# A mixture-of-experts kernel whose per-tile expert weights are copied by VectorE instead of by SyncE's transfers

## The chip, the cores and the metric

The kernel runs on one NeuronCore of one Trainium2 chip. The metric is the device time of one launch in microseconds. The kernel before has three timed runs: 1335.67, 1336.54 and 1336.85 us, a median of 1336.54.

## The reference, cut to what matters

Six layers work on a residual stream x of 4096 tokens with 128 features, in float32: a mixture of experts with gelu, a state-space layer, the gelu mixture again, a mixture with swiglu, an attention layer of the RWKV kind, and the swiglu mixture again. The changed code is that of the mixtures:

```
gelu mixture   (8 experts, 2 of them for each token, F = 512):
  h      = gelu(x @ w1[e] + b1[e])          w1[e]: 128 x 512
  y      = h @ w2[e] + b2[e]                w2[e]: 512 x 128
swiglu mixture (8 experts, 2 of them for each token, I = 256):
  h      = silu(x @ w1[e].T) * (x @ w3[e].T)   both 128 x 256 as the kernel holds them
  y      = h @ w2[e].T                         256 x 128
each: out = sum over a token's two experts of gate * y
```

The kernel computes only the two chosen experts of a token.

## The kernel before

**Mixtures.** `mixture` is called three times: for the first gelu layer, for the second gelu layer and the first swiglu layer together (the merged layer: a gelu stage, then a swiglu stage), and for the last swiglu layer. Each stage cuts its 32 groups of 128 tokens into four parts (of 4, 12, 12, 4 groups in the first layer; 4, 12, 8, 8 and 8, 12, 8, 4 in the merged one; 8, 12, 8, 4 in the last). For each part VectorE normalises the tokens (`stats`, `normalise`), TensorE computes the gate's logits, VectorE picks two experts for each token and computes a place for each token and choice in a sorted list (`route`, `places`), and GpSimd sends the tokens to their places in DRAM, one indirect transfer of 128 rows for each group and choice (`send`, L1190). The list of a part is padded so that a tile of 128 places has one expert. `table` packs the experts of the tiles into words, eight 3-bit digits in each, one word per iteration.

**Products.** A stage has 92 tiles, in 23 iterations of BODY = 4 tiles; the loops are unrolled by two iterations (`run`), but iterations that have work beside the products stand alone, outside the loops. In each tile TensorE multiplies the tile's tokens, transposed in halves of an iteration (`turn_set`, L602), by the expert's first weights (`first_products`, four matmuls, L611) into one of four PSUM banks `hb`; ScalarE applies gelu (L708) or silu (L712), for swiglu VectorE multiplies by the other half (`multiply`, L952); and two tiles later TensorE multiplies by the second weights (`second_products`, four or two matmuls, L622), which it reads straight from the expert's place in the table. After two tiles VectorE takes the outputs from PSUM (`output`: L961 with a bias for gelu, L963 for swiglu) and ScalarE stores them to DRAM (L718). Later GpSimd fetches each token's two results back, an indirect transfer each (`fetch`, L1199), and ScalarE and VectorE weigh and sum them (`scale_lower`, `combine` with L997 and L1003, `norm`, `finish`).

**Where the first weights come from.** The matmul's weights stand in a buffer `weights` of four tiles. SyncE fills it: for each tile it works out the expert from a word of the table (L503) and issues a transfer from the table in SBUF to the buffer, also in SBUF (`fill`, L507, 128 partitions by 516 floats for gelu, with the bias, or 512 for swiglu). It waits until the tile's slot is free: after gelu (`hid_ready`), or after the first products (`h_ready`). In an iteration SyncE issues the four fills of the next iteration, and then the load of the tokens of the iteration after that (`load`, L499), which waits for the transposes of this iteration and, at a part's first tiles, for that part's sends (`sent`):

```
for j in range(BODY):
    sp.wait_ge(used_of[kinds[now]], i * BODY + (j + 1 + BANKS))
    sp.sem_inc(held, 1)
    fill(j, experts[j], kinds[fills])
...
    load(i + 2, loading)
```

**Who else does what beside the products.** The tables `beside` say at which tile of which iteration each engine does its share of the routing and combining; the change leaves them as they are. On VectorE they stand in its queue between the multiplies and outputs.

## Time and profile before

| What | Value |
|---|---|
| Median of three runs | 1336.54 us |
| Span of the profiled execution | 1697.2 us |
| Busy: TensorE, its weight loads | 1114.7 us, 926.2 us |
| Busy: VectorE, ScalarE, GpSimd | 765.2 us, 553.5 us, 751.0 us |
| Moved by the DMA engines | 199.71 MB, 118 GB/s on average |
| Fills of `weights` (L507) | 184 of 258 KB and 184 of 256 KB |
| Loads of tokens (L499) | 92 of 256 KB |

The profiled execution is one of its own, with the profiler recording it; its span, from the first to the last instruction, is all that is known of its time, and it is 361 us longer than the median of the unrecorded runs. Busy time on one engine lies beside that of others. The state-space layer and the attention layer lie at about 380 to 475 us and 1100 to 1358 us of the span; the product loops of the mixtures at 47 to 345 us, 494 to 1079 us (its swiglu stage from 797), and 1402 to 1675 us.

### The profile page before, as it was taken

The numbers are of one execution on the slowest core, as the hardware profiler recorded it, in microseconds if no ns is written. First come the engines' busy times: TensorE is split into PE (matmuls) and PEld (weight loads), VectorE is DVE, ScalarE is ACT, GpSimd is POOL, SyncE is SP. The second block draws the span as 40 slices with busy tenths as digits, with TensorE's granted clock in tenths as the row PEclk, the third lists the DMA queues.
The fourth block names the chain that finished last, engine by engine and source line by source line (L and its number), as shares of the span: only waits on it lengthen the run. The fifth ranks groups of instructions, "written<-read, shape, count | busy, mean of one in ns | idle before, by whom it ended". The sixth has DMA issues, their size and how long they took to land. (4 is left out here: it accounts for less than half of the span.)

```text
span 1697.2 us, 28236 instructions
## 1 busy us (share of the span) xinstructions
PE 1114.7 (66%) x6835; PEld 926.2 (55%) x6836; DVE 765.2 (45%) x2839; ACT 553.5 (33%) x1653; POOL 751.0 (44%) x802
## 2 busy tenths in 40 slices
PE   2376888437656699867477548289799734768482
PEld 2375888434346588757376547234344334657372
DVE  5221324158671133544146313269979762335132
ACT  1133546247413255533032113134343301223131
POOL 3634263521054625545715552255645456442522
PEclk9787999678966799978688769589999955879696
DMA  8544567310023345544354436100000003445363
GB/s 251 169 143 138 183 197 245 109 41 1 0 81 111 130 165 196 181 133 139 109 198 159 140 118 205 53 0 1 1 0 0 0 29 127 165 152 203 117 208 106
DMA packets 198792, 199.71 MB, mean 118 GB/s; under 512 B 22212, under 2 KB 140310, under 8 KB 198678
## 3 DMA queue, kind: packets, MB, share of 16 engines
q1 hardware_dynamic: 123138, 136.22, 23.5%
q0 software_dynamic: 16384, 33.59, 6.6%
q10 hardware_dynamic: 59156, 28.57, 5.9%
q8 instruction: 48, 0.79, 0.2%
q14 instruction: 66, 0.54, 0.1%
HBM read 52.44 MB, written 49.02 MB: 60 GB/s over the span
## 5 line engine op out<-in xcount | busy, mean ns | idle before, releaser
L611 PE MATMUL gelu_hb<-gelu_xsT,gelu_weights 128*128 128x128 f32 x2208 | 340.1, 298 | 65.5 <-issue 61.3
L611 PEld LDWEIGHTS gelu_hb<-gelu_xsT,gelu_weights 128*128 128x128 f32 x2208 | 308.7, 213 | 75.4 <-issue 73.5
L708 ACT ACTIVATE gelu_hid<-gelu_hb,gelu_weights 128x128 f32<-128x128 f32 x736 | 208.8, 374 | 238.6 <-remote 127.1
L1190 POOL DMA_INDIRECT slots_x<-gelu_xn,gelu_index x176 | 172.4, 980 | 203.6 <-DVE gelu_index L921 154.2
L622 PE MATMUL gelu_ob<-w,gelu_hid 128*128 x1472 | 220.0, 292 | 43.8 <-issue 41.5
L961 DVE TENSOR_TENSOR gelu_ys<-gelu_ob,bias 128x128 f32<-128x128 f32 x184 | 51.7, 291 | 392.4 <-PE gelu_ob L622 176.1
L622 PEld LDWEIGHTS gelu_ob<-w,gelu_hid 128*128 128x128 f32 x1472 | 198.7, 206 | 51.4 <-issue 51.1
L611 PE MATMUL swiglu_hb<-swiglu_xsT,swiglu_weights 128*128 128x128 f32 x736 | 114.8, 302 | 27.3 <-issue 27.2
L611 PEld LDWEIGHTS swiglu_hb<-swiglu_xsT,swiglu_weights 128*128 128x128 f32 x736 | 104.2, 217 | 29.0 <-issue 29.0
L952 DVE TENSOR_TENSOR gelu_hid<-gelu_sil,gelu_hb 128x256 f32<-128x256 f32 x92 | 38.4, 419 | 151.9 <-ACT gelu_sil L712 82.0
L952 DVE TENSOR_TENSOR swiglu_hid<-swiglu_sil,swiglu_hb 128x256 f32<-128x256 f32 x92 | 38.5, 419 | 149.3 <-ACT swiglu_sil L712 72.8
L602 PE MATMUL gelu_turn<-ident,gelu_xs 128*128 128x128 f32 x276 | 62.3, 311 | 65.8 <-ACT gelu_xsT L701 25.6
L1851 POOL TENSOR_TENSOR rwkv_tw<-rwkv_tw,rwkv_qr 128x512 f32<-128x512 f32 x64 | 79.5, 1275 | 53.4 <-DVE rwkv_tw L1810 44.4
L701 ACT COPY gelu_xsT<-gelu_turn 128x256 f32<-128x256 f32 x138 | 52.2, 378 | 150.9 <-remote 87.6
L1190 POOL DMA_INDIRECT slots_x<-swiglu_xn,swiglu_index x64 | 62.7, 980 | 81.0 <-DVE swiglu_index L921 62.9
L622 PE MATMUL gelu_ob<-s,gelu_hid 128*128 x368 | 66.3, 309 | 47.3 <-issue 27.3
L712 ACT ACTIVATE gelu_sil<-gelu_hb 128x256 f32<-128x256 f32 x92 | 35.1, 383 | 168.2 <-remote 87.8
L622 PE MATMUL swiglu_ob<-s,swiglu_hid 128*128 x368 | 64.6, 304 | 36.1 <-issue 22.8
L712 ACT ACTIVATE swiglu_sil<-swiglu_hb 128x256 f32<-128x256 f32 x92 | 34.9, 383 | 161.8 <-PE swiglu_hb L611 78.2
L622 PEld LDWEIGHTS gelu_ob<-s,gelu_hid 128*128 128x128 f32 x368 | 56.2, 219 | 50.6 <-issue 50.6
L1199 POOL DMA_INDIRECT raw_s<-slots_y,gelu_index x72 | 69.0, 959 | 21.7 <-issue 18.7
L602 PEld LDWEIGHTS gelu_turn<-ident,gelu_xs 128*128 128x128 f32 x276 | 36.2, 158 | 75.5 <-issue 30.1
(375 smaller groups left out, 1997.1 us busy)
## 6 DMA issues: line engine op xcount, KB each, us to landing
gelu_weights<-w SPq DMA_DIRECT2D x184, 258.0 KB
gelu_weights<-s SPq DMA_DIRECT2D x92, 256.0 KB
swiglu_weights<-s SPq DMA_DIRECT2D x92, 256.0 KB
gelu_xs<-slots_x SPq DMA_DIRECT2D x69, 256.0 KB
slots_y<-gelu_ys ACTq DMA_DIRECT2D x138, 128.0 KB
swiglu_xs<-slots_x SPq DMA_DIRECT2D x23, 256.0 KB
slots_y<-swiglu_ys ACTq DMA_DIRECT2D x46, 128.0 KB
slots_x<-zeros SPq DMA_DIRECT2D x2, 1984.0 KB
```

Of the source, the lines that this page charges most:

```text
L602: last = pe.transpose(turn[:, j * P:(j + 1) * P], xs[:, odd * BODY + half * SET + j, :], ident[:, :])
L611: last = pe.matmul(hb[j][:, c * P:(c + 1) * P], weights[:, j, c * P:(c + 1) * P], xsT[j // SET][:, j % SET, :], start=True, stop=True)
L622: last = pe.matmul(o, hid[:, r, c * P:(c + 1) * P], w2[:, bass.ds(e, 1), c, :].rearrange("p a d -> p (a d)"), start=c == 0, stop=c == CH[k ...
L701: act.copy(xsT[half][:, :, :], turn[:, 0:SET * P].rearrange("p (j d) -> p j d", j=SET)).then_inc(set_ready, 1)
L708: last = act.activation(hid[:, j % RING, c * P:(c + 1) * P], hb[j][:, c * P:(c + 1) * P], ACT.Gelu, bias=weights[:, j, FF + c:FF + c + 1])
L712: act.activation(sil[:, j, :], hb[j][:, 0:FI], ACT.Silu).then_inc(sil_ready, 1)
L952: dve.tensor_tensor(hid[:, j % RING, 0:FI], sil[:, j, :], hb[j][:, FI:2 * FI], ALU.mult).then_inc(hid_ready, 1)
L961: dve.tensor_tensor(y, o, res["bias"][:, bass.ds(es[n] * D, D)], ALU.add).then_inc(y_done, 1)
L1190: pool.indirect_dma_start(slots_x[:, :], bass.IndirectOffsetOnAxis(index[p][:, k, g:g + 1], 0), tokens[p][:, g, :], None).then_inc(sent[p] ...
L1199: pool.indirect_dma_start(back[p][k][:, g, :], None, slots_y[0:(SLOT0[p] + PART_TILES[p]) * P, :], bass.IndirectOffsetOnAxis(index[p][:, k ...
L1851: pool.tensor_tensor(T(b, 2), tw[b][:, j % 2, 0:TILE], q["r"][b][:, :], ALU.mult).then_inc(S["m_done"], 1)
```

## The change

VectorE fills `weights`, with a copy from the table, also in SBUF. The buffer has eight slots in place of four, one half for each of two successive iterations: in iteration i, ahead of its multiply of tile j, VectorE copies the weights of tile j of iteration i+1 to the other half. It waits for the tile four before its own (`hid_ready` or `h_ready` at s + 1) and counts each copy in one semaphore `weights_copied`, for which TensorE waits. VectorE reads the words for that, three for two iterations of a loop (one before, and only where gelu outputs need a bias). The iteration before a new stage stands alone too, and VectorE passes the wait for a part's table an iteration earlier. The first four copies of a layer stand between `stats(2)` and `route(1)`. SyncE no longer reads words or fills; it only loads tokens, with the same waits for transposes and sends. To make room, silu writes into the ring `hid` (so ScalarE waits for the second products of the tile four before), VectorE multiplies there in place, the buffer `sil` is gone, and in the first layer `back_small` lies in `s2`, which is filled only later. The semaphore for the first layer's weights is split into one for w1 with its bias and one for w2.

```diff
+    sp.dma_start(res["w1"][:, :, 0:FF], ins["L0_ffn_w1"].rearrange("e d f -> d e f")).then_inc(later["w1_in"], 16)
+    sp.dma_start(res["w1"][:, :, FF:WIDE], ins["b1_columns"]).then_inc(later["w1_in"], 16)
...
-        weights = L.sb("weights", [P, BODY, WIDE if any_gelu else FF])
+        weights = L.sb("weights", [P, HELD, WIDE if any_gelu else FF])
         hid = L.sb("hid", [P, RING, FF if any_gelu else FI])
-        sil = L.sb("sil", [P, BANKS, FI]) if any_swiglu else None
...
-        small = L.sb("back_small", [P, TOP * PART_GROUPS[0], D])
+        small = res["s2"][:, 0:TOP * PART_GROUPS[0], :] if begun else L.sb("back_small", [P, TOP * PART_GROUPS[0], D])
...
+                alone = [0, ITERS - 1, *ITER0[1:-1], *(k - 1 for k in ITER0[1:-1])]
...
-            def experts_of(i):
-                word = sp.value_load(words[0:1, bass.ds(i, 1)], min_val=0, max_val=E ** DIGITS - 1)
-                return [sp.snap((word >> (3 * (LAG + j))) & (E - 1), min_val=0, max_val=E - 1) for j in range(BODY)]
-
-            def fill(j, e, kind):
-                sp.dma_start(weights[:, j, 0:WIDTH[kind]], table_of[kind][:, bass.ds(e, 1), :].rearrange("p a f -> p (a f)")).then_inc(weights_ready[j], 16)
-
-            def body(i, stages, needs=None, loads=True):
-
-                now, fills, loading = stages
-                experts = experts_of(i + 1)
-                for j in range(BODY):
-                    sp.wait_ge(used_of[kinds[now]], i * BODY + (j + 1 + BANKS))
-                    sp.sem_inc(held, 1)
-                    fill(j, experts[j], kinds[fills])
...
+            def body(i, stage, needs=None):
                 if needs:
                     sp.wait_ge(sent[needs], SENT[needs])
-                    sp.wait_ge(table_ready, needs + 1)
-                if loads:
-                    sp.wait_ge(turned, i * 2 + 2)
-                    sp.wait_ge(loaded, i * 16 + 32)
-                    sp.sem_inc(held, 1)
-                    load(i + 2, loading)
+                sp.wait_ge(turned, i * 2 + 2)
+                sp.wait_ge(loaded, i * 16 + 32)
+                sp.sem_inc(held, 1)
+                load(i + 2, stage)
...
-                pe.wait_ge(weights_ready[j], i * 16 + 16)
+                pe.wait_ge(weights_copied, s + 1)
                 pe.wait_ge(hid_ready, s + 1)
                 for c in range(FF // P):
-                    last = pe.matmul(hb[j][:, c * P:(c + 1) * P], weights[:, j, c * P:(c + 1) * P], xsT[j // SET][:, j % SET, :],
+                    last = pe.matmul(hb[j][:, c * P:(c + 1) * P], weights[:, odd * BODY + j, c * P:(c + 1) * P], xsT[j // SET][:, j % SET, :],
...
+                act.wait_ge(out_ready, s + 1)
                 if kind == "gelu":
...
-                    act.activation(sil[:, j, :], hb[j][:, 0:FI], ACT.Silu).then_inc(sil_ready, 1)
+                    act.activation(hid[:, j % RING, 0:FI], hb[j][:, 0:FI], ACT.Silu).then_inc(sil_ready, 1)
...
-                dve.wait_ge(out_ready, s + 1)
-                dve.tensor_tensor(hid[:, j % RING, 0:FI], sil[:, j, :], hb[j][:, FI:2 * FI], ALU.mult).then_inc(hid_ready, 1)
+                h = hid[:, j % RING, 0:FI]
+                dve.tensor_tensor(h, h, hb[j][:, FI:2 * FI], ALU.mult).then_inc(hid_ready, 1)
...
+            def fill(slot, e, kind):
+                dve.tensor_copy(weights[:, slot, 0:WIDTH[kind]], table_of[kind][:, bass.ds(e, 1), :].rearrange("p a f -> p (a f)"))\
+                   .then_inc(weights_copied, 1)
+            def words_of(i, turns):
+                return [word_at(i + n) for n in range(turns + 1)]
+            def body(i, first, last, beside, ready, now, was, then):
+                word, u, odd = ready
+                ahead = None if last else [expert_in(word[u + 1], LAG + j) for j in range(BODY)]
                 for j in range(BODY):
                     s = i * BODY + j
+                    if not last:
+                        if not first:
+                            dve.wait_ge(hid_ready if was == "gelu" else h_ready, s + 1)
+                            dve.sem_inc(held, 1)
+                        fill((1 - odd) * BODY + j, ahead[j], then)
...
+            dve.wait_ge(table_ready, 1)
+            if first_in:
+                dve.wait_ge(first_in, 32)
+            dve.sem_inc(held, 1)
+            word = word_at(0)
+            for j in range(BODY):
+                fill(j, expert_in(word, LAG + j), kinds[0])
...
-            run(dve, body, beside, {upto(p): (lambda p=p: await_table(p)) for p in with_words}, experts_of)
+            run(dve, body, beside, {upto(p) - 1: (lambda p=p: await_table(p)) for p in range(1, NPARTS)}, words_of)
```

## Rows read from the trace of the kernel before

The windows view has: stretch, its length, busy us of each engine (instructions in brackets), granted clock, DMA share, GB/s. The timeline has: start us, length us, engine, line, operation, tiles, count, and the idle time before it with what ended it. A group has: line, engine, operation, tiles, shapes, count, busy us, mean ns of one, idle us before it and what ended it. A source line has: count, ns least/median/most, first and last start.

**Rows 1.** The page: its first line.
```profile
span 1697.2 us, 28236 instructions
```

**Rows 2.** A stretch of the windows view; one matmul of the timeline.
```profile
1360.00:1396.00 36.00, 14.78 (x66) 13.68 (x67) 23.57 (x165) 4.21 (x6) 18.81 (x17) 0.51 0.08 26
...
1007.14 0.37 PE L611 MATMUL gelu_hb<-gelu_xsT,gelu_weights 128*128 128x128 f32 x1 [2.44 <-issue]
```

**Rows 3.** The timeline, a gelu iteration's ends, then a swiglu one's.
```profile
206.64 1.06 PE L611 MATMUL gelu_hb<-gelu_xsT,gelu_weights 128*128 128x128 f32 x8
...
214.22 1.06 PE L611 MATMUL gelu_hb<-gelu_xsT,gelu_weights 128*128 128x128 f32 x8
...
1017.21 0.61 PE L622 MATMUL gelu_ob<-s,gelu_hid 128*128 x4
...
1017.82 0.42 DVE L952 TENSOR_TENSOR gelu_hid<-gelu_sil,gelu_hb 128x256 f32<-128x256 f32 x1 [1.03 <-PE gelu_ob L622]
...
1018.16 0.42 DVE L963 COPY gelu_ys<-gelu_ob 128x256 f32<-128x256 f32 x1
...
1023.00 0.61 PE L622 MATMUL gelu_ob<-s,gelu_hid 128*128 x4
```

**Rows 4.** Groups of L602 by form; then what readers of gelu_weights waited for.
```profile
L602 PE MATMUL gelu_turn<-ident,gelu_xs 128*128 128x128 f32 x276 | 62.3, 311 | 65.8 <-ACT gelu_xsT L701 25.6 <-DMA gelu_xs<-slots_x 21.5 <-issue 16.5
...
L602 PE MATMUL swiglu_turn<-ident,swiglu_xs 128*128 128x128 f32 x92 | 21.1, 316 | 39.8 <-ACT swiglu_xsT L701 27.2 <-issue 9.0 <-DMA swiglu_xs<-slots_x 3.3
...
  DMA gelu_weights<-w: 0.3, 1
```

**Rows 5.** The page's DMA queues: kind, packets, MB, share of 16 engines.
```profile
q1 hardware_dynamic: 123138, 136.22, 23.5%
...
q0 software_dynamic: 16384, 33.59, 6.6%
```

**Rows 6.** VectorE over 128x512: two groups by form, and a pair in the timeline.
```profile
L1481 DVE TENSOR_SCALAR ssm_dt<-ssm_dt,floor 128x512 f32<-128x512 f32 x8 | 3.7, 478 | 2.2 <-ACT ssm_dt L1413 1.9
...
L1467 DVE TENSOR_SCALAR ssm_dt<-ssm_bank_a,laT 128x512 f32<-128x512 f32 x8 | 5.7, 748 | 0.2
...
413.77 0.86 DVE L1481 TENSOR_SCALAR ssm_dt<-ssm_dt,floor 128x512 f32<-128x512 f32 x2
```

**Rows 7.** L969, VectorE's reading of a word: ns least/median/most.
```profile
L969 DVEq TENSOR_LOAD <-gelu_words x47: 300/309/1224, 54.3 to 793.2; - x47
...
L969 DVEq FUSED_REGOPS  x47: 190/190/216, 55.6 to 793.5; - x47
```

**Rows 8.** The windows view of three product stages.
```profile
494.00:797.00 303.00, 226.76 (x1711) 216.68 (x1710) 106.88 (x561) 131.12 (x447) 149.50 (x160) 0.85 0.45 149
...
797.00:1079.00 282.00, 175.83 (x1218) 164.26 (x1216) 107.33 (x420) 60.33 (x169) 132.23 (x153) 0.78 0.46 151
...
1402.00:1675.00 273.00, 172.94 (x1238) 162.45 (x1238) 88.88 (x331) 58.17 (x162) 112.21 (x130) 0.78 0.49 160
```

**Rows 9.** The group of the gelu output's bias, by form.
```profile
L961 DVE TENSOR_TENSOR gelu_ys<-gelu_ob,bias 128x128 f32<-128x128 f32 x184 | 51.7, 291 | 392.4 <-PE gelu_ob L622 176.1 <-remote 109.5 <-DMA gelu_back_small<-slots_y,gelu_index 84.5
```

**Rows 10.** L1190, L833, L1773 and L1789 by source line; two neighbours in the timeline.
```profile
L1190 POOL DMA_INDIRECT slots_x<-gelu_xn,gelu_index x176: 954/964/1291, 28.1 to 968.9; - x176
...
L833 DVE TENSOR_SCALAR gelu_xn<-x,gelu_mv,gelu_rstd x88: 327/341/559, 12.3 to 925.9; 128x128 f32<-128x128 f32 x88
...
L1773 DVE SCALAR_TENSOR_TENSOR raw_s<-raw_s,laT,rwkv_xT x8: 741/743/747, 1113.4 to 1241.0; 128x512 f32<-128x512 f32 x8
...
L1789 DVE SCALAR_TENSOR_TENSOR raw_s<-rwkv_qr,laT,rwkv_qk x8: 741/1358/4289, 1140.3 to 1268.1; 128x512 f32<-128x512 f32 x8
...
940.84 0.69 DVE L1003 SCALAR_TENSOR_TENSOR x<-gelu_xn,x 128x512 f32<-128x512 f32 x1
...
941.13 1.27 POOL L1190 DMA_INDIRECT slots_x<-gelu_xn,gelu_index  x1 [0.28 <-issue]
```

**Rows 11.** The timeline, the last layer's first step of route(1).
```profile
1385.25 0.26 DVE L844 COPY swiglu_lg<-swiglu_ob 128x96 f32<-128x96 f32 x1 [0.89 <-PE swiglu_ob L586]
```

More of the change, by code:

```diff
@@ L466, in mixture, with run @@
         group = lambda t, p: t[:, COL0[p]:COL0[p] + PART_GROUPS[p]]
[L468 removed]
+        def run(eng, body, beside, breaks=(), prepare=lambda i, turns: None):
             i = 0
@@ L624, in second_products, with word_of @@
                 last.then_inc(out_ready, 1)
-            def word_of(i, _needed):
+            def word_of(i, _turns):
                 return pe.value_load(words[0:1, bass.ds(i, 1)], min_val=0, max_val=E ** DIGITS - 1)
-            def body(i, first, last, beside, ready, now, was):
+            def body(i, first, last, beside, ready, now, was, then):
                 word, u, odd = ready
@@ L733, in copy_tokens, with body @@
                 act.copy(xT[:, n % XT, :], early[p][q][:, :]).then_inc(xt_copied, 1)
-            def body(i, first, last, beside, _ready, now, was):
+            def body(i, first, last, beside, ready, now, was, then):
+                _, _u, odd = ready
                 for j in range(BODY):
@@ L983, in body @@
                 if last:
-                    output(NTILES // SET - 1, 1, ITERS - 1, experts[BODY:BODY + SET], now)
+                    es = [expert_in(word[u], BODY + n) for n in range(SET)] if now == "gelu" else None
+                    output(NTILES // SET - 1, 1, ITERS - 1, es, now)
             def await_table(p):
```

77 lines of the change are left out of this document (31 added, 46 removed).

## Prediction, made before the changed kernel was run

> **What bounds the kernel now.** I read the page first: the profiled execution spans 1697.2 us [rows 1], but the three runs shown have a median of 1336.5 us. Recording made this execution 361 us longer, so I had to find where. The timeline shows it: while GpSimd issues its indirect transfers, single matmuls of 0.37 us stand up to 2.44 us apart and wait for "issue", that is, for nothing that the profile shows [rows 2]. The same happens between 1360 and 1396 us, where the DMA engines are busy 8% of the time [rows 2], so the weight transfers aren't needed for it. I take these gaps for the recording's own. The sum below is therefore a difference between two executions, put on the median; a share of the 1697.2 us would count the gaps as work.
>
> In the clean stretches TensorE sets the pace. In a swiglu stretch the second products of the first tile of two successive iterations start at 1017.21 and 1023.00: 5.79 us for four tiles, with nothing waited for between [rows 3]. In a gelu stretch the first products of the same tile start at 206.64 and 214.22: 7.58 us [rows 3].
>
> What does TensorE wait for in them? Not for the weights: over the whole span its first products waited 0.3 us, once, for a weight transfer [rows 4]. It waits for tokens: its transposes stood 21.5 + 3.3 = 24.8 us behind the tokens' load [rows 4], since SyncE issues that load behind four weight transfers, each of which waits for a tile of the iteration. The weight transfers are cheap in time yet not in traffic: 368 of 128 partitions by 512 or 516 floats are 96.8 MB of the 136.22 MB of SyncE's queue [rows 5].
>
> The second limit is GpSimd. Its queue moves 33.59 MB in indirect transfers of 128 rows of 512 bytes [rows 5], so 512 of them, at 0.96 us each with 0.3 us before the next [rows 10], or about 650 us of work, and a part of the tokens isn't loaded until its sends are done. In the two gelu layers the second part has 24 sends (30 us) beside 12 ready tiles (23 us at 7.58 us for four), so TensorE waits there; and so it does where sends of later parts come late.
>
> **Part by part.**
>
> *The fills move to VectorE.* 368 copies of 128x516 or 128x512. The nearest row is the tensor_scalar from SBUF to SBUF over 128x512, 478 ns, and two of them in a row take 0.86 us, so 0.43 us each [rows 6]. The one that reads PSUM takes 748 ns [rows 6]; that is the upper bound. Nothing makes a copy cheaper than 0.43 - I take 0.43, since source and target are in SBUF here too. In all 368 x 0.43 = 158 us of VectorE work (275 at the upper bound). It costs nothing as long as VectorE has the room; so the room is what must be priced.
>
> *The words.* VectorE reads three words per two iterations: 1.5 x (0.31 + 0.19) = 0.75 us an iteration [rows 7], where it read half a word in the gelu stage and none in the swiglu stage. Working out an expert takes two register operations for each fill; I put 0.1 us on each, an estimate (they partly run ahead), so 0.4.
>
> *Room in the swiglu stages.* Before, VectorE's own work in four tiles is four multiplies and two copies that start 0.34 us apart [rows 3]: 2.04 us of 5.79. After it: 2.04 + 4 x 0.43 + 0.75 + 0.4 = 4.9 us, so 0.9 us stay free, 23 x 0.9 = 21 us in a stage. The work beside the products (combines, norms, routing) is VectorE's busy time less multiplies and copies (92 x 0.42 + 46 x 0.42 = 58 us): 107.33 - 58 = 49 us in the merged layer's swiglu stage, 88.88 - 58 = 31 us in the last layer [rows 8]. What exceeds the room is 28 and 10 us. TensorE can't run ahead of it: a tile's second products need its multiply two tiles later. In the merged layer some of it falls into waits for GpSimd's sends, which hide about a third. I charge 18 + 10 = **+28 us**; bounds 0 (all in such waits) and 97 (nothing hidden, and each fill at the PSUM price: 38 + 184 x 0.32).
>
> *Room in the gelu stages.* Own work: 4 x 0.29 [rows 9] + 1.72 + 0.75 + 0.4 = 4.0 of 7.58 us. Beside it 106.88 - 92 x 0.29 = 80 us in the merged layer's stage [rows 8], 3.5 us an iteration, so it just fits; bunches of it will cost **+4** (0 to 15).
>
> *GpSimd beside the fills.* An indirect transfer has a median of 964 ns; the one that started while VectorE was in a 0.69 us operation on two SBUF inputs took 1.27 us [rows 10]. So an SBUF operation of VectorE can hold GpSimd 0.3 us. A fill is shorter; I take 0.1 us for each of some 400 transfers issued beside fills, 40 us of GpSimd, of which the part before a late part of the tokens counts, about a quarter: **+10** (0 to 60, below).
>
> *Routing behind the first fills.* Four fills and a word, 2.2 us, now stand ahead of route(1), whose sends are late in the gelu layers. In the last layer VectorE idled 0.89 us there [rows 11]. **+2** for three such places, since the gelu layers have slack behind it or the same idle time (0 to 4). New waits in VectorE's queue: a fill waits for tile s-4, long done; the wait for the first weights ends before; and the wait for a part's table is for VectorE's own earlier work. What queues behind each fill is the multiply and the output copy, priced above.
>
> *SyncE.* The load of iteration i+2 is issued as soon as iteration i is transposed, about an iteration earlier, so the 24.8 us of token waits go, save for those that really end with a part's sends: **-20** (-25 to 0). After such a stall the weights are in place, where before four transfers of half a microsecond's issue followed; five such restarts, 1 us each: **-5** (-10 to 0). ScalarE writes silu into the ring and waits for second products four tiles back: nothing.
>
> Sum: 28 + 4 + 10 + 2 - 20 - 5 = +19, so 1336.5 + 19 = about 1355 us. What is late next: the multiply (VectorE) in swiglu stages.
>
> **Rivals.**
>
> *A. The transfers were the hidden cost (faster).* Without the fills SyncE's queue moves 39 MB where it moved 136. The clean stretches say little of the stretches in which indirect transfers compete, since the recording spoils them. If there loads and stores of tokens were late by 0.7 us in each of the 92 iterations, that is 64 us more to gain; with the sum above: 1355 - 64 = about 1291. The point that decides: the gain in those stretches must exceed 19 us, 0.2 us an iteration. For: four fills, a load and two stores are 1.57 MB in 5.79 us, 272 GB/s, before a send adds to it. Against: 0.3 us of waiting for weights [rows 4]. If it is half of that, 1323.
>
> *B. VectorE and GpSimd shut each other out (slower still).* In the attention layer the same 128x512 operation on two SBUF inputs takes 744 ns alone and 1358 ns beside GpSimd's tensor operations, up to 4289 [rows 10]. If each fill holds off an indirect transfer for all its 0.43 us, it is 158 us of GpSimd, and a quarter counts, 40 in place of 10; GpSimd's own operations hold up fills too, some 15 us more: 1355 + 30 + 15 = 1400. Against: VectorE's normalising of tokens, much of it beside the sends, has a median of 341 ns and never took over 559 [rows 10]. The Trainium skill (SBUF — State Buffer, "SBUF: two separate sides") says that fp32 copies within SBUF take a port pair that GpSimd needs for writing descriptors, an exclusive lock for the whole instruction. By that rule the 1400 is due; the 1.27 us row supports a lock, though for 0.3 us only.
>
> *C. All of it in the waits for GpSimd (no change).* If the sends alone set the time of the merged layer, both excess and gain vanish in them, and 10 + 10 in the last layer against its tokens' share cancel: 1336.
>
> **How the numbers follow.** My forecast (VectorE becomes the bound of the swiglu stages) gets 0.45, B 0.10, A 0.38, C 0.07. A difference under 0.2%, 2.7 us, can't be told from none. Slower: 0.45 + 0.10 = 0.55; faster 0.38; same 0.07. The forecast's own range is 1340 to 1385; A reaches from 1280 to 1333, B to 1410. Since both signs have weight, the range takes both in: 1290 to 1400 leaves out 0.1 below and 0.1 above.
>
> **What would show it.** Right: a fill of about 0.45 us; VectorE's busy time up by some 170 us; in the swiglu stages idle time of second products put down to the VectorE multiply; no wait of the transposes for the tokens' load; iterations there of 6.3 us or more on average. Rival A: the clean iterations stay at 5.79, and the time beside sends shrinks. B: indirect transfers of 1.2 us and more as the rule. What would make the prediction wrong: register work and word loads that run ahead at no cost give back 20 us or more, and a TensorE that waited in the unrecorded runs for transfers that this trace can't show.

## The result, and the profile after

The changed kernel takes 1347.73 us (median of 4 runs, 1344.26 to 1349.38), the kernel before 1336.11 us (4 runs beside them): a ratio of 1.0079, 95% interval 1.0057 to 1.010, so 11.6 us slower. The prediction said slower, 1355 us, range 1290 to 1400. Later, beside other kernels, the changed kernel took 1346.74 us (6 runs), 1.0073 times the kernel before (1.0046 to 1.0099); 1345 to 1350 had been expected if the 11.6 us were the change's own. Medians and ratios are of the fast runs alone, which leaves out two runs of `ring8_ahead`, of 1787 and 2595 us.

The page of the changed kernel: its first line, busy time by engine, DMA packets and two queues.

```profile
span 1342.5 us, 28059 instructions
...
PE 1022.4 (76%) x6835; PEld 861.5 (64%) x6836; DVE 907.0 (68%) x3207; ACT 555.5 (41%) x1653; POOL 770.9 (57%) x802
...
q1 hardware_dynamic: 70146, 39.35, 10.1%
q0 software_dynamic: 16384, 33.59, 8.3%
```

Against [rows 1] the span is 355 us shorter, though the kernel is slower. So the first thing to clear up was the recorded execution of before, and the kernel before was recorded once more. The page of that second recording:

```profile
span 1337.6 us, 28236 instructions
...
PE 1017.8 (76%) x6835; PEld 852.1 (64%) x6836; DVE 767.6 (57%) x2839; ACT 559.1 (42%) x1653; POOL 751.9 (56%) x802
...
q1 hardware_dynamic: 123138, 136.22, 29.9%
```

It spans 1337.6 us, within 0.2% of the medians of the unrecorded runs (the time of this very execution is 1339.4 us). All comparisons from here on are with it. What the 1697 us were is told at the end.

SyncE's queue moves 39.35 MB where it moved 136.22 ([rows 5] and here), VectorE is busy 139 us longer, GpSimd 19 us. Where does the kernel lose its 11.6 us? Second products run from the start of each stage of products to its end, so their first and last start give its length. The view by source line, first after, then the second recording of before (count, ns least/median/most, first to last start):

```profile
L599 PE MATMUL gelu_ob<-w,gelu_hid x1472: 274/275/578, 51.5 to 632.6; 128*128 x184
L599 PE MATMUL gelu_ob<-s,gelu_hid x368: 274/275/578, 633.6 to 827.0; 128*128 x184
L599 PE MATMUL swiglu_ob<-s,swiglu_hid x368: 274/275/577, 1157.6 to 1317.9; 128*128 x184
```

```profile
L622 PE MATMUL gelu_ob<-w,gelu_hid x1472: 275/275/422, 51.6 to 632.0; 128*128 x184
L622 PE MATMUL gelu_ob<-s,gelu_hid x368: 275/275/575, 633.0 to 827.6; 128*128 x184
L622 PE MATMUL swiglu_ob<-s,swiglu_hid x368: 275/275/372, 1157.7 to 1311.9; 128*128 x184
```

The two kernels run level until the last layer. There the stage takes 1317.9 - 1157.6 = 160.3 us, where it took 154.2. That doesn't mean that nothing happened in the others: gains and losses cancel in the merged layer. The waits of TensorE show both (us in total, times, longest; "issue" is idle time for which the profile shows no releaser). After:

```profile
PE gelu_turn L579 <- DMA gelu_xs<-slots_x: 35.2, 5, 10.1
...
PE gelu_ob L599 <- DVE gelu_hid L930: 19.2, 13, 3.6
...
PE gelu_ob L599 <- DVE gelu_ys L939: 9.5, 4, 6.5
PE swiglu_ob L599 <- DVE swiglu_hid L930: 8.3, 11, 2.3
...
PE gelu_hb L588 <- issue: 4.9, 2, 2.5
```

Before, in its second recording:

```profile
PE gelu_turn L602 <- DMA gelu_xs<-slots_x: 60.5, 25, 15.2
...
PE gelu_hb L611 <- issue: 7.8, 1, 7.8
...
PE swiglu_turn L602 <- DMA swiglu_xs<-slots_x: 7.4, 11, 1.2
...
PE gelu_ob L622 <- DVE gelu_hid L952: 6.5, 9, 1.6
...
PE swiglu_ob L622 <- DVE swiglu_hid L952: 1.2, 3, 0.6
```

Read them in pairs. Waits of the transposes for the tokens' load: 60.5 + 7.4 = 67.9 us before, 35.2 after; the many short ones are gone (36 waits then, 5 now), what is left ends with a part's sends. Waits of second products for VectorE's multiply: 7.7 us before, 27.5 after. In the merged layer's swiglu stage the two cancel (tokens 29.8 to 15.2, multiply 6.5 to 19.2), in the last layer there is less to give back (7.4 to 0, against 1.2 to 8.3). The trace gives 4.9 us of the difference between the spans, the medians 11.6: the changed kernel's recorded execution was the fastest of its four, and the recorded one of before was 2 us above the median. The second recording of after spans 1346.3 us, with stages within 0.4 us of the first one's. The stages together are only 4 us longer than before in either recording of after, so about 7 of the 11.6 us of the medians can't be placed in a stage by these recordings.

What VectorE now does, by source line: L951 copies weights, L944 reads a word.

```profile
L951 DVEq ALU_OP  x736: 45/45/58, 37.4 to 1310.0; - x184
L951 DVEq FUSED_REGOPS  x368: 57/57/71, 37.5 to 1310.1; - x184
L951 DVE COPY gelu_weights<-w x184: 409/430/1900, 37.7 to 613.7; 128x516 f32 x184
L951 DVE COPY gelu_weights<-s x92: 411/427/636, 619.3 to 819.2; 128x512 f32 x92
...
L944 DVEq FUSED_REGOPS  x184: 190/190/216, 37.0 to 1311.6; - x184
L944 DVEq SEQ_ASSERT  x184: 23/23/35, 37.3 to 1311.8; - x184
L944 DVEq TENSOR_LOAD <-gelu_words x138: 298/307/954, 36.5 to 820.3; - x138
L944 DVEq TENSOR_LOAD <-swiglu_words x46: 298/309/912, 1135.1 to 1311.2; - x46
```

A copy takes 0.43 us, as [rows 6] had it. The words are the surprise: 138 + 46 = 184 readings in 92 iterations, two in each, where the prediction counted one and a half. An iteration with routing, norms or combines beside it stands alone, one that stands alone reads two words, and a loop needs four free iterations in a row. The count says that VectorE has no loop left: two words in each of 92 iterations, less one in the last iteration of each of the three layers, and one ahead of each layer's first copies, is 184. Each costs VectorE's sequencer 0.31 + 0.19 + 0.02 = 0.52 us, 96 us in all (24 before, 47 readings). The register operations for the experts are another 736 x 0.045 + 368 x 0.057 = 54 us.

### The profile page after: what moved, and what is told of

The parts are those of the page before. It is cut to its first block and busy times, and to the rows that moved or that the text cites. A ratio compares the mean times of both kernels' runs of the same rounds, so it can differ in the third digit from the quotient of the medians.

```text
span 1342.5 us, 28059 instructions
## 1 busy us (share of the span) xinstructions
PE 1022.4 (76%) x6835; PEld 861.5 (64%) x6836; DVE 907.0 (68%) x3207; ACT 555.5 (41%) x1653; POOL 770.9 (57%) x802
## 3 DMA queue, kind: packets, MB, share of 16 engines
q1 hardware_dynamic: 70146, 39.35, 10.1%
## 5 line engine op out<-in xcount | busy, mean ns | idle before, releaser
L588 PE MATMUL gelu_hb<-gelu_xsT,gelu_weights 128*128 128x128 f32 x2208 | 308.8, 286 | 4.9 <-issue 4.9
L588 PEld LDWEIGHTS gelu_hb<-gelu_xsT,gelu_weights 128*128 128x128 f32 x2208 | 285.1, 202 | 5.3 <-issue 5.3
L599 PE MATMUL gelu_ob<-w,gelu_hid 128*128 x1472 | 200.1, 281 | 9.8 <-DVE gelu_ys L939 9.5
L599 PEld LDWEIGHTS gelu_ob<-w,gelu_hid 128*128 128x128 f32 x1472 | 184.3, 197 | 11.0 <-issue 10.9
L951 DVE COPY gelu_weights<-w 128x516 f32 x184 | 85.5, 483 | 65.5 <-issue 39.3
L588 PE MATMUL swiglu_hb<-swiglu_xsT,swiglu_weights 128*128 128x128 f32 x736 | 100.6, 282 | 0.0
L579 PE MATMUL gelu_turn<-ident,gelu_xs 128*128 128x128 f32 x276 | 57.5, 293 | 40.1 <-DMA gelu_xs<-slots_x 35.2
L1808 DVE TENSOR_TENSOR_SCAN rwkv_tw<-rwkv_qd,rwkv_carry,rwkv_bank_a 128x512 f32<-128x512 f32 x64 | 76.8, 1274 | 0.0
L599 PE MATMUL gelu_ob<-s,gelu_hid 128*128 x368 | 61.5, 293 | 19.5 <-DVE gelu_hid L930 19.2
L689 ACT ACTIVATE swiglu_hid<-swiglu_hb 128x256 f32<-128x256 f32 x92 | 35.2, 383 | 83.8 <-PE swiglu_hb L588 64.7
L1156 POOL TENSOR_TENSOR gelu_rstd<-gelu_ve,neg_half 128x4 f32<-128x4 f32 (+2 forms) x12 | 20.0, 1666 | 86.1 <-DVE gelu_ve L804 85.9
L689 ACT ACTIVATE gelu_hid<-gelu_hb 128x256 f32<-128x256 f32 x92 | 35.2, 383 | 82.1 <-PE gelu_hb L588 68.5
```

The source lines that it names most:

```text
L579: last = pe.transpose(turn[:, j * P:(j + 1) * P], xs[:, odd * BODY + half * SET + j, :], ident[:, :])
L588: last = pe.matmul(hb[j][:, c * P:(c + 1) * P], weights[:, odd * BODY + j, c * P:(c + 1) * P], xsT[j // SET][:, j % SET, :], start=True, s ...
L599: last = pe.matmul(o, hid[:, r, c * P:(c + 1) * P], w2[:, bass.ds(e, 1), c, :].rearrange("p a d -> p (a d)"), start=c == 0, stop=c == CH[k ...
L689: act.activation(hid[:, j % RING, 0:FI], hb[j][:, 0:FI], ACT.Silu).then_inc(sil_ready, 1)
L951: dve.tensor_copy(weights[:, slot, 0:WIDTH[kind]], table_of[kind][:, bass.ds(e, 1), :].rearrange("p a f -> p (a f)"))\
L1808: dve.tensor_tensor_scan(tw[b][:, j % 2, 1:TILE + 1], q["d"][b][:, :], bank_a[b][:, :], carry[b][:, j:j + 1], ALU.mult, ALU.add).then_inc( ...
```

## The experiments

Theory at the outset: VectorE's added work costs some 30 us or more, mostly in the swiglu stages, and SyncE's earlier token load gives 20 back. Rivals: the early load gives nothing; the transfers themselves had a price (the prediction's A); the silu in the ring, the extra stand-alone iterations or GpSimd cost the time. Times are medians, with the ratio to the kernel before on the same chip. The ratios differ from the quotient of the two medians by up to 0.13%, 2 us; where a conclusion hangs on it, both are given. The last four columns are lengths of product stages in one recorded execution (first to last start of second products, as above); the merged swiglu stage is counted from the gelu stage's end.

| kernel | us | ratio (95%) | layer 1 | merged gelu | merged swiglu | last |
|---|---|---|---|---|---|---|
| before, again | 1337.1 | 1 | 204.1 | 221.6 | 195.6 | 154.2 |
| after, again | 1346.7 | 1.0073 (1.0046-1.0099) | 203.0 | 222.3 | 194.0 | 160.1 |
| load_first | 1353.5 | 1.0110 (1.0086-1.0133) | 206.7 | 223.3 | 196.1 | 158.7 |
| ring8_sync | 1337.9 | 1.0000 (0.9982-1.0019) | 199.6 | 218.8 | 199.7 | 156.7 |
| half_fills | 1332.2 | 0.9957 (0.9939-0.9975) | 202.5 | 223.0 | 189.9 | 154.6 |
| load_late | 1346.5 | 1.0073 (1.0048-1.0098) | 204.7 | 223.9 | 191.9 | 159.4 |
| fewer_words | 1335.4 | 0.9991 (0.9974-1.0008) | 203.4 | 222.3 | 191.7 | 151.7 |
| multiply_first | 1334.9 | 0.9991 (0.9978-1.0005) | 203.1 | 222.4 | 190.7 | 150.6 |
| ring8_fills_first | 1324.7 | 0.9903 (0.9875-0.9931) | 198.4 | 216.6 | 193.4 | 153.7 |
| ring8_ff_half | 1316.7 | 0.9866 (0.9844-0.9887) | 196.4 | 215.7 | 191.0 | 149.6 |
| ring8_ahead | 1333.0 | 0.9976 (0.9960-0.9992) | 199.8 | 218.3 | 192.4 | 157.1 |

What a recorded execution spends outside the four stages lies between 558 and 567 us. This scatter is as large as many of the differences: of the 8.7 us between the spans of "before, again" and "after, again" 3.9 lie in the stages and 4.8 outside them. Two recordings of the changed kernel differ by at most 0.4 us in a stage. So the stages say where the products take longer, and the medians by how much the kernel does.

**before_again.** The kernel before, unchanged.

> The kernel before, unchanged, recorded once more. If the long span (1697.2 us recorded against 1336.5 us unrecorded) belongs to the recording of a kernel whose fills are transfers of SyncE, it comes again: a span of 1600 us or more, with single matmuls up to 2 us apart, since the recording of the changed kernel, without those transfers, spans 1342.5 us, no longer than its unrecorded time. If it was a chance of that one recording, the span is now within 1% of 1336 us. The unrecorded time stays at 1336 us within 0.2%.

The span is 1337.6 us. The long first recording had nothing to do with how this kernel is recorded. The single execution was 1339.38 us, the 23 runs of the kernel before beside it had a median of 1337.06.

**load_first.** The kernel before, with the tokens' load ahead of the fills.

```diff
+                def tokens_of():
+                    sp.wait_ge(turned, i * 2 + 2)
+                    sp.wait_ge(loaded, i * 16 + 32)
+                    sp.sem_inc(held, 1)
+                    load(i + 2, loading)
+
+                if loads and not needs:
+                    tokens_of()
                 for j in range(BODY):
                     sp.wait_ge(used_of[kinds[now]], i * BODY + (j + 1 + BANKS))
                     sp.sem_inc(held, 1)
                     fill(j, experts[j], kinds[fills])
```

> The kernel before, with one edit: SyncE issues the tokens' load of iteration i+2 ahead of the four fills of iteration i+1, not behind them (in the four or so iterations that wait for a part's sends it stays behind). Theory (the earlier load gives back 20 us, VectorE's work costs 30 or more): 1316 us, 1311 to 1325. Rival (the wait for tokens is one for a part's sends, whatever SyncE does; the load was never late): 1336 us within 2.7. Under the rival the +11.6 us measured are the price of VectorE's work by itself.

1353.5 us: 16.5 slower than before by the medians, 14.7 by the ratio, where the theory had 20 gained and the rival nothing. Both fall. TensorE's waits, and below them one of SyncE's:

```profile
PE gelu_turn L607 <- DMA gelu_xs<-slots_x: 41.9, 5, 14.4
PE gelu_hb L616 <- issue: 18.2, 7, 8.8
PE gelu_hb L616 <- DMA gelu_weights<-w: 6.9, 5, 2.6
PE swiglu_hb L616 <- DMA swiglu_weights<-s: 4.0, 4, 2.3
PE gelu_hb L616 <- DMA gelu_weights<-s: 3.9, 4, 1.3
...
SPq L517 <- DMA gelu_xs<-slots_x: 19.5, 11, 3.0
```

The token waits did shrink, from 67.9 to 43.0 us (41.9 and 1.1 in the last layer), 25 us as the theory had it. In their place first products wait: 6.9 + 4.0 + 3.9 = 14.8 us for weights, where the second recording of before shows none, and 21.2 for "issue" (18.2 and 3.0 in the last layer), where it shows 8.1. SyncE's own wait shows why: L517 is its wait for the load before, up to 3.0 us, and four fills now stand behind it. With four slots a fill can't be issued until its tile is used, so it has no slack to lose.

**ring8_sync.** The changed kernel, with SyncE's transfers in place of VectorE's copies: load first, then four fills.

```diff
+                if loads and not needs:
+                    tokens_of()
+                for j in range(BODY):
+                    sp.wait_ge(hid_ready if kinds[was] == "gelu" else h_ready, i * BODY + (j + 1))
+                    sp.sem_inc(held, 1)
+                    sp.wait_ge(weights_ready[j], i * 16 + 16)
+                    sp.sem_inc(held, 1)
+                    fill((i + 1) & 1, j, experts[j], kinds[fills])
```

> The changed kernel, but SyncE fills the eight slots with transfers, tokens first, and VectorE copies nothing and reads no more words than before. Everything else of the change stays: silu into the ring hid, eight slots, first fills a layer earlier against w1, iterations that stand alone. Theory (VectorE's copies and words cost, the load gains): 1310 to 1320 us, 28 to 38 below the changed kernel, and no different from load_first by more than 3 us. Rival (transfers cost time in the bus or in GpSimd's sends, and the copies are cheap): 1345 us or more. Rival (silu in the ring, or the iterations that stand alone, cost the time): about 1347 minus at most 5.

1337.9 us, the time of before, and 9 us faster than the changed kernel. It keeps silu in the ring, the stand-alone iterations, the earlier first fills and `back_small` in `s2`, so these can't be what makes the changed kernel slower; that they cost nothing at all isn't shown, since the eight slots may hide a cost. It is 16 us better than load_first, which has four slots and the same order of load and fills. But it isn't the 1310 to 1320 of the theory: the fills still go out in a burst behind the load, and first products still wait 5.1 us for weights in the merged layer and 1.5 in the last, and 18.7 for "issue".

**half_fills.** The changed kernel; a copy moves 256 of 512 floats. It leaves out half of the weights, so its outputs are wrong and only its time is of use.

```diff
+                at = 0 if whole else WIDTH[kind] - FF // 2
-                dve.tensor_copy(weights[:, slot, 0:WIDTH[kind]], table_of[kind][:, bass.ds(e, 1), :].rearrange("p a f -> p (a f)"))\
+                dve.tensor_copy(weights[:, slot, at:WIDTH[kind]], table_of[kind][:, bass.ds(e, 1), at:WIDTH[kind]].rearrange("p a f -> p (a f)"))\
```

> The changed kernel; all fills but the first four of a layer copy the second half of the first products' weights alone (256 of 512 floats), so the first products of half of the hidden units use stale weights. VectorE has some 360 times 0.2 us = 72 us less to do, nothing else changes. Theory (VectorE's time is what costs, and a third of it or so shows): 8 to 15 us faster than the changed kernel, 1333 to 1340 us, with less idle time of second products put down to the VectorE multiply. Rival (the waits come from the words and register work ahead of each iteration, or from GpSimd, not from copying): within 3 us of 1347.7.

1332.2 us, 14.5 below the changed kernel: at the upper end of the theory, though the copies shrank by less than expected (a mean of 0.31 us for 128x256 in the last layer where a whole one has 0.46, 41 us of VectorE's busy time in all). The part of the gain that the recording shows lies in the swiglu stages, 4.1 and 5.5 us; the gelu stages don't move. The prediction had put the room there: enough in the gelu stages, too little in the swiglu ones. Two cautions. GpSimd's busy time fell too, by 11 us (770.9 to 759.9), so what the copies cost through GpSimd is in the 14.5 as well. And the waits of second products for the multiply fell only from 27.5 to 23.7 us, less than the 9.6 us of the two stages: that row points at the place, but it doesn't measure the cost.

**load_late.** The changed kernel, with SyncE's load held back to where it stood.

```diff
+                sp.wait_ge(hid_ready if kinds[now] == "gelu" else h_ready, i * BODY + (BODY + BANKS))
+                sp.sem_inc(held, 1)
                 if needs:
                     sp.wait_ge(sent[needs], SENT[needs])
                 sp.wait_ge(turned, i * 2 + 2)
```

> The changed kernel, but SyncE's load of iteration i+2 waits until the fourth tile of iteration i is used, as it did before, when it stood behind the fills. So the change without its earlier load. Theory (the earlier load gives back some 20 us where no transfers of weights stand in its way; in load_first it only pushed the fills back): waits of transposes for the load rise from 35 us to about 60, time 1360 us, 1353 to 1367. Rival (an early load gains nothing in any kernel, as load_first suggests, since without fills the load is short enough even late): 1347 within 3.

1346.5 us against 1346.7: no difference. The rival holds, and the prediction's reason for its largest gain falls. The transposes wait 37.0 us for tokens here and 35.2 in the changed kernel, so a late load is in time when no weights go ahead of it. An early load shortened these waits too in load_first (to 43.0), but there it cost more than it gave; in the changed kernel it is the missing transfers that shorten them, and the earlier load adds next to nothing.

**fewer_words.** The changed kernel; swiglu iterations don't read the word that they don't use.

```diff
-                return [word_at(i + n) for n in range(turns + 1)]
+                return [word_at(i + n) if n or outputs else None for n in range(turns + 1)]
```

> The changed kernel; in swiglu iterations VectorE doesn't read the word that only gelu outputs need: two words for two iterations in place of three, 23 readings of 0.3 + 0.2 us less in 46 iterations, 11 us of VectorE's queue. Nothing else changes. Theory (VectorE's queue as a whole, reading of words and register work included, is what costs; halving the copies took 15 us off with 40 to 70 us of work): 2 to 5 us faster than the changed kernel. Rival (the sequencer reads ahead while the engine copies, so words cost nothing): within 1.5 us of it.

1335.4 us: 11.3 us gained, the whole of what the change had cost, and more than the theory's 2 to 5. The expectation had also counted wrongly, one word in two iterations: the kernel makes 139 readings where it made 184. So 45 readings of 0.52 us, 23 us of VectorE's sequencer, are worth 11.3 us of the kernel. VectorE's waits show the same place. In the changed kernel, then with this edit:

```profile
DVE swiglu_weights L951 <- PE swiglu_hb L588: 14.4, 14, 2.2
...
DVE swiglu_weights L951 <- issue: 11.4, 14, 1.5
```

```profile
DVE swiglu_weights L951 <- issue: 6.2, 14, 1.0
DVE swiglu_weights L951 <- PE swiglu_hb L588: 4.7, 10, 0.7
```

VectorE stood idle 14.4 + 11.4 = 25.8 us ahead of the last layer's copies and now stands 10.9. The name behind the arrow misleads: the copy waits for first products four tiles back, done long ago, and nothing about them changed. It was the sequencer, reading words.

**multiply_first.** fewer_words, with the multiply ahead of the copy.

```diff
-                        fill((1 - odd) * BODY + j, ahead[j], then)
                     if now == "swiglu":
                         multiply(s, j)
+                    if not last:
+                        fill((1 - odd) * BODY + j, ahead[j], then)
```

> fewer_words with one more edit: in swiglu iterations VectorE multiplies tile j before it copies the weights of tile j of the next iteration, not after. The work is the same. Theory (VectorE is late by its amount of work in bunches, so the order of copy and multiply matters little): 1335.4 us within 3. Rival (a copy ahead of the multiply delays the second products by its own 0.43 us, latency and not amount): 1325 us or less. Rival (the copy fills the time in which VectorE waits for silu, 35 us of idle time in the two stages, and behind the multiply it no longer does): 1340 us or more.

1334.9 us against 1335.4, the same ratio. The amount of VectorE's work counts, not which of the two comes first. Both rivals fall.

**ring8_fills_first.** ring8_sync with its two halves exchanged: the fills of iteration i+1 go out as their slots come free during iteration i-1, the load of i+2 behind them.

```diff
-                if loads and not needs:
-                    tokens_of()
                 for j in range(BODY):
...
                     fill((i + 1) & 1, j, experts[j], kinds[fills])
...
+                if loads:
                     tokens_of()
```

> SyncE fills the eight slots by transfers, as in ring8_sync, but each fill of iteration i+1 goes out as soon as its tile of iteration i-1 is used, and the load of iteration i+2 behind them, at the start of iteration i. So neither stands in the way of the other, and VectorE copies nothing. Theory (in load_first and ring8_sync the early load's gain of 20 to 26 us was lost again in weights that came late behind it): both waits go, 1320 us, 1315 to 1328. Rival (the transfers themselves, 97 MB, cost time wherever they stand): 1335 us or more, as ring8_sync.

1324.7 us, 0.9903 of the kernel before: faster than both. It keeps the changed kernel's eight slots and leaves the filling with SyncE. Against ring8_sync only the order in the queue differs, and it is worth 13 us. Weights are late once, for 0.4 us. The transposes still wait 45.8 + 5.5 = 51.3 us for tokens, so of the theory's two waits only one went. Two stages and two waits:

```profile
L629 PE MATMUL gelu_ob<-w,gelu_hid x736: 274/276/422, 404.8 to 621.4; 128*128 x184
...
L629 PE MATMUL swiglu_ob<-s,swiglu_hid x368: 274/276/422, 1142.7 to 1296.4; 128*128 x184
...
PE gelu_turn L609 <- DMA gelu_xs<-slots_x: 45.8, 9, 15.1
...
PE gelu_hb L618 <- DMA gelu_weights<-s: 0.4, 1, 0.4
```

**ring8_ff_half.** The same with transfers of half the width. Like half_fills it leaves out half of the weights.

```diff
+                at = 0 if whole else WIDTH[kind] - FF // 2
-                sp.dma_start(weights[:, bass.ds(half * BODY + j, 1), 0:WIDTH[kind]].rearrange("p a f -> p (a f)"),
-                             table_of[kind][:, bass.ds(e, 1), :].rearrange("p a f -> p (a f)")).then_inc(weights_ready[j], 16)
+                sp.dma_start(weights[:, bass.ds(half * BODY + j, 1), at:WIDTH[kind]].rearrange("p a f -> p (a f)"),
+                             table_of[kind][:, bass.ds(e, 1), at:WIDTH[kind]].rearrange("p a f -> p (a f)")).then_inc(weights_ready[j], 16)
```

> ring8_fills_first with every transfer but those of a layer's first two iterations moving the second half of the first products' weights alone (half of the hidden units use stale weights): 48 MB less traffic, the same number of transfers. Theory (once the transfers are issued early enough they cost nothing): 1324.7 us within 3. Rival (the traffic itself delays tokens, sends and stores, a hidden cost): 1318 us or less, and then removing all of it would be worth over 12 us.

1316.7 us, ratio 0.9866 (0.9844 to 0.9887) against 0.9903 (0.9875 to 0.9931). The two were timed on different chips, and the intervals overlap slightly, but each is set against the kernel before beside it, and all four stages are shorter by 1 to 4 us, 9.4 in all. This is the rival's side: the traffic has a price even where no first product waits for weights, for half of it 8 us by the medians and 5 by the ratios. If the other half costs as much (not tried), 10 to 16 us in all. The windows view of 130 us of the last layer, first ring8_fills_first, then this one, has the load in its last columns (granted clock, DMA share, GB/s):

```profile
1155.00:1285.00 130.00, 121.59 (x1024) 116.59 (x1023) 74.53 (x288) 48.84 (x136) 83.38 (x98) 0.99 0.82 266
```

```profile
1155.00:1285.00 130.00, 121.35 (x1044) 117.16 (x1042) 75.59 (x292) 50.02 (x138) 87.91 (x102) 1.00 0.67 200
```

The engines that move data are busy 82% of the time at 266 GB/s with whole transfers, and TensorE gets 1024 matmuls done in a stretch in which it gets 1044 done with half ones. (The stretches don't lie equally far into the stage; in the first 130 us of each one's stage it is 1027 and 1067.) The waits don't say how the traffic costs this time: the transposes wait 51.3 us for tokens with whole transfers and 50.3 with half ones. Of the 9.4 us in the stages 5.4 appear as busy time of TensorE, 672.3 against 666.9 us for the same number of matmuls. Why they take longer stays open.

**ring8_ahead.** ring8_fills_first; where SyncE waits for a part's sends, it first issues the fills of the iteration that needs them.

```diff
                 if needs:
-                    sp.wait_ge(sent[needs], SENT[needs])
                     sp.wait_ge(table_ready, needs + 1)
+                    sp.sem_inc(held, 1)
+                    fills_of(i + 1, stage_of_iter(i), loading)
+                    sp.wait_ge(sent[needs], SENT[needs])
```

> ring8_fills_first; in the seven places where SyncE waits for a part's sends, it first issues the four fills of the iteration that needs these tokens, which it otherwise issues behind the load. Theory (after such a wait the first products stand for weights, 7.9 us once in the first layer): 1320 us, 1316 to 1323. Rival (the wait is the sends' own, and weights were in time): 1324.7 within 2. Rival (those fills wait for the tiles of the iteration two before, so that a load which could go early goes late): 1328 us or more.

1333.0 us, 8 slower (10 by the ratios): the third possibility. Those fills wait until iteration i is used, and the load stands behind them, where it could have gone an iteration earlier. The waits fit: the transposes wait 61.0 us for tokens where they waited 51.3, and in the last layer 11.9 where they waited 5.5. No run tested this alone.

**act_fills.** ring8_fills_first, with ScalarE copying in the swiglu stages.

```diff
                     nonlinear(s, j, odd, now)
+                    if filling:
+                        act.copy(weights[:, (1 - odd) * BODY + j, 0:FF], res["s13"][:, bass.ds(ahead[j], 1), :].rearrange("p a f -> p (a f)"))\
+                           .then_inc(weights_ready[j], 16)
```

> ring8_fills_first, but in the swiglu stages ScalarE copies the weights on chip, each copy behind its silu of the same tile, and reads the words for it; the gelu stages keep SyncE's transfers. ScalarE was busy 61 of 194 us there, VectorE 105. Theory (transfers cost about 16 us in all by ring8_ff_half, half of it in the swiglu stages, and an engine with room can take the copies): 1317 us, 1312 to 1322. Rival (ScalarE's copies and words make the silu late, and second products wait for it as they waited for VectorE's multiply): 1330 us or more.

1698.8 us, beside 1710.5 us for the kernel before on the same chip: ratio 0.9925 (0.99 to 0.9951). On this chip the kernel before took 1.28 times as long as elsewhere, so the expected microseconds can't be compared, and a ratio from here says little of the others. That it beats the kernel before here is shown; whether it beats ring8_fills_first stays open.

## Why the prediction was right, and where it was not

The direction was right, and the size was 19 us for 11.6. The cost was VectorE's, as the prediction said, though less of it in the swiglu stages and more in the gelu ones; the gain was about as large as it said, for another reason, and that part is luck. The sum, by its own steps:

**VectorE in the swiglu stages, +28: right in place, some 20 in size.** Second products wait for the multiply 20 us more than before (27.5 - 7.7), halving the copies gave back 14.5 us and dropping the unused words of these stages 11.3. No run measures the 28 by itself. The nearest comparison is with ring8_fills_first, which has the same slots and no copies on VectorE: the changed kernel's two swiglu stages are 0.6 + 6.4 = 7 us longer, and if its missing transfers give back twice what half of them do there (2.4 + 4.1), VectorE's part is 7 + 13 = 20 us. The working had two errors that offset each other. Words were undercounted (1.04 us an iteration by 2 x 0.52, not 0.75), and so was register work (54 / 92 = 0.59, not 0.4). A copy costs less than 0.43 when other work stands beside it, since its neighbour starts before it ends: in the timeline of "after, again" one starts at 1237.23 and the next instruction at 1237.57, 0.34 us later. That is the quickest case; the mean busy time of a copy in the last layer is 0.46. Together 4 x 0.34 + 1.04 + 0.59 = 3.0 us an iteration, against 1.72 + 0.75 + 0.4 = 2.9 in the prediction. For the same reason VectorE's busy time rose by 139 us and not by 170; these are 1.5 us an iteration, and with them in place of 4 x 0.34 it is 3.1.

**The gelu stages, +4: too little.** They take 203.0 and 222.3 us where they took 204.1 and 221.6, which looks like nothing. But in ring8_fills_first they take 198.4 and 216.6, so what moved to VectorE costs 10 us in them, and some 16 if the missing transfers give back twice what half of them do (2.0 + 0.9); the eight slots hide it in the comparison with before. That they had the room for the copies holds (half_fills changes nothing in them); which of the words, the register work and GpSimd takes the time there no run separates.

**GpSimd beside the copies, +10: too much, and not separated.** Indirect transfers of before and of after:

```profile
L1190 POOL DMA_INDIRECT slots_x<-gelu_xn,gelu_index x176: 954/963/1291, 27.9 to 761.7; - x176
```

```profile
L1188 POOL DMA_INDIRECT slots_x<-gelu_xn,gelu_index x176: 954/970/1412, 28.2 to 766.9; - x176
```

The median hardly moves, single ones stretch, the longest of any to 1.6 us. In all GpSimd is busy 19 us longer (751.9 to 770.9), 0.05 us for each copy, where 40 were put down; 13 of the 19 lie in the 512 indirect transfers. By the prediction's own quarter that would be 5 us. No run changed this alone.

**Routing behind the first fills, +2: not seen.** The stages' second products start at 51.5, 410.2 and 1157.6 us, where they started at 51.6, 410.4 and 1157.7. What it may do to later sends no run separates.

**The earlier load, -20, and restarts, -5: the step that failed.** The prediction said that token waits come from SyncE, "since SyncE issues that load behind four weight transfers", and that issuing it as soon as iteration i is transposed makes them go. The order in the queue was right, the remedy was not. In the changed kernel an early and a late load cost the same (load_late), and in the kernel before an early one lost 16.5 us (load_first). The token waits fell by 33 us, 31 of them with a load as late as before, because 97 MB of transfers went. That is the prediction's rival A in kind: moving the weights by DMA had a hidden cost. In size it isn't. A asked for over 19 us beyond the sum and wrote down 64; halving the traffic gives 5 to 8, which makes some 10 to 16 for all of it, in place of the -25 and not on top of it. The -5 had no run of its own; "issue" waits ahead of first products fell from 8.1 to 4.9 us.

**The first profile.** The sentence that the gaps between single matmuls are "the recording's own" was wrong. A recorded execution of either kernel spans what an unrecorded one takes. [Rows 2 and 3] come from an execution with the marks of those on the chip of act_fills. The clean iterations of [rows 3] do hold elsewhere (first products of one tile in two successive iterations start at 1194.91 and 1200.77 in the second recording of before, 5.86 us), and this saved the sum: it was built from durations in clean stretches and set on the median. What the long recording hid was the price of transfers: it moved 160 GB/s in the last layer's stage, which in the second recording runs at 268, and showed 24.8 us of token waits in place of 67.9 [rows 4, 8].

**How the parts add up.** From ring8_fills_first, which has no copies on VectorE and weights late only once: 1324.7. Taking its transfers away would give 10 to 16 us, to 1309 at the least. The changed kernel is at 1346.7, so VectorE's copies, words and register work cost about 38 us by the medians, GpSimd's part in it, and 33 by the ratios (the stages of the recordings give 36, 20 in the swiglu and 16 in the gelu stages; the prediction said 44 with GpSimd and routing). Against the kernel before, by the medians, VectorE costs 38; the transfers that are gone give back 16; and the eight slots with their better order give 11 (1336 to 1325), a term that the prediction didn't have. 38 - 27 = +11. That this comes out is no check, since the 38 was reckoned from the other two; what carries it is the step from half the traffic to all of it, which no run took.

**Rival B** fell: a copy has a median of 0.43 us and the indirect transfers one of 0.97, not 1.2 and more. The Trainium skill (SBUF — State Buffer, "SBUF: two separate sides") has every such copy shut GpSimd out of descriptor writing for its whole length. If GpSimd were always at it, 368 x 0.43 = 158 us would be missing there, and 19 are; the stretched single transfers fit such a lock, but no run tests it. **Rival C** fell with the ratio's interval.

## What to carry to other kernels

Before moving a transfer to an engine, count everything in its instruction stream that the copy needs: here reading words and computing addresses (96 + 54 us of the sequencer) is as much work as the copies, and one unused word in each swiglu iteration cost as much as the whole change. A buffer that is refilled only once its tile is used makes the order in the issuing queue decide; here doubling the slots and issuing first what is free early made the kernel before 11 us faster, without moving the copying at all. And when a recorded execution is far from the unrecorded time, record it again before reading waits from it.

## What had not been expected of the hardware

The same kernel runs 1.28 times as long on one chip as on the three others of the experiments: 1710.5 us (11 runs, 1704 to 1718) where they give medians of 1336 to 1337. The kernel before's first recording, 1697.2 us, has the same marks. From the recording of act_fills there, its span and TensorE's largest waits:

```profile
span 1701.1 us, 28113 instructions
...
PE gelu_ob L629 <- issue: 63.7, 63, 3.5
PE gelu_hb L618 <- issue: 60.6, 62, 2.9
PE swiglu_turn L609 <- ACT swiglu_xsT L708: 41.5, 4, 18.6
```

Some 120 gaps ahead of products wait for nothing that the profile shows, where the second recording of before has, ahead of first products, one of 7.8 us and one of 0.3. The mean granted clock was 0.81 in it and 0.89 in the second recording of before. What slows that chip, and whether the lower clock is cause or result of the gaps, stays open.

Reading one word into a register costs VectorE's queue 0.31 + 0.19 + 0.02 = 0.52 us, and the profile books it to no engine's busy time. It shows as idle time ahead of the next instruction, in part under a releaser that had long been done: with 45 readings fewer this idle time in the last layer fell from 25.8 to 10.9 us.
